# Two-layer conditional network on one core: the first loads divided between two DMA queues

## The chip, the cores and the metric

The kernel runs on one core of one Trainium2 chip. The metric is the device time of that core in microseconds (us), the median of several runs. TensorE (PE) multiplies matrices, VectorE (DVE), ScalarE (ACT) and GpSimd (POOL) work on elements, SyncE (SP) issues DMAs. ScalarE can issue DMAs too, on a queue of its own.

## What is computed

There are 4 batches of 512 tokens of width 256, and for each batch a vector of 8 numbers, `cond_8`. The first layer mixes eight weight matrices by these numbers, masks the mix and adds its result to x. The second layer is a mixture of experts with one shared expert; `cond_8` also picks and weighs two of the eight experts of a batch.

```python
# first layer, per batch b
masked_w = weight * mask[None, :, :]                 # 8 x 256 x 256
w_bot = jnp.einsum('bg,got->bot', y, masked_w)       # y = cond_8
x = x + jnp.einsum('bnt,bot->bno', x, w_bot) + bias
# second layer
w, sel = top_k(softmax(cond_8), 2); w = w / w.sum()
mlp = lambda x, g, u, d: (gelu(x @ g) * (x @ u)) @ d # 256 -> 1024 -> 256
x = x + sum(w[k] * mlp(x, *skill[sel[k]]) for k in (0, 1)) + mlp(x, *shared)
```

## The kernel before, in words

Everything is kept transposed: the 256 features lie in two halves (`hh`, `oh`) of 128 partitions, the 512 tokens of a batch along the free dimension. Each fp32 operand of a matmul is split into a high part (a cast to fp32r) and a low part (the rest), and a product is three matmuls. The high parts are cast by ScalarE, the low parts are formed by VectorE (x, h and the first-layer weight) or GpSimd (the weights of the second layer). An expert's weights are eight chunks of 128 x 768: 256 columns each for gate, up and down. The second layer walks over 24 chunks a batch (8 shared, 16 routed), `gate_up` two steps ahead of `down`. The order of the work of each engine is written out by hand, with semaphores between them.

Batch 0 has a way of its own ahead of these steps, and this is where the change lies:

- SyncE issues all big loads. Its list ahead of the batches (L218 to L231) is: weights 0 and 1 of the first layer (`l0_raw`, 256 KB each, L186), half 0 of x (`x_in`, 256 KB, L174), weights 2 and 3, half 1 of x, weights 4 to 7, two halves of the mask (L228), the eight chunks of the shared expert (`raw`, 384 KB each, L230), then, behind a wait for the splits of batch 0's x (L178), the x of batch 1. Each weight, each half of x and each chunk has a semaphore of its own.
- ScalarE issues one tiny load, `cond_row` (L469), copies `ident` (L471, with a table load ahead of it), scales `ident` by each of batch 0's eight numbers (`scale_ident`, L424, into `diag`, which lies in `out_sb`), casts the two halves of x (`split_x`, L401), loads the table for gelu (L481), casts the two halves of the mixed weight (`split_l0_0`, L405) and goes on to the shared chunks (`split_part`, L421).
- TensorE keeps itself busy with matmuls of zeros (`keep_warm`, L371), spreads `cond` over the partitions (L376), and mixes the second output halves of the eight weights with the scaled identities (`mix_l0`, L248). Between weights 5 and 6 it passes x through to the sum (`pass_x`, L256 and L258). Then come the first layer's own matmuls (`first_layer_0`, L266 and L270) and the second layer.
- VectorE mixes the first output halves of the weights, one instruction a weight (`combine_0`, L550 for weight 0 and L553), in the order 0 to 4, low part of x half 0 (L593), 5, low part of x half 1, 6, 7. Then it applies the masks (`apply_mask_0`, L563) to its own half and to TensorE's.

Weights of the first layer stay in `l0_raw` for all batches, so they are loaded once.

Of the kernel before, what the change touches and what calls it, by code (L numbers as in the profile page):

```python
# [25 lines left out]

def build(nc, xT, cond, l0_w, l0_mask, experts, shared, outT):
    B, _, HH, T = xT.shape
    G = l0_w.shape[0]
    E, CHUNKS, _, WC = experts.shape  # L30
    D = HH * P
    L0C = HH * D
# [14 lines left out]
    with ExitStack() as ctx:  # L47
        def sb(name, shape, dt=F32):
            return ctx.enter_context(nc.sbuf_tensor(name, shape, dt))
# [4 lines left out]
        def sem(name):  # L54
            return ctx.enter_context(nc.semaphore(name))
# [22 lines left out]
        l0_raw = sb("l0_raw", [P, G, L0C])  # L78
# [4 lines left out]
        x_in = sb("x_in", [P, HH, T])  # L83
# [39 lines left out]
        l0_in = [sem(f"l0_in{g}") for g in range(G)]  # L123
        mask_in = [sem(f"mask_in{oh}") for oh in range(HH)]
        x_loaded = [sem(f"x_loaded{hh}") for hh in range(HH)]
# [45 lines left out]
        @block.sync  # L171
        def _(sp):
            def load_x_half(b, hh):
                sp.dma_start(x_in[:, hh], xT[bass.ds(b, 1), :, hh].rearrange("a p t -> (a p) t")).then_inc(x_loaded[hh], 16)  # L174

            def load_x(b):
                if isinstance(b, int) and b == 1:
                    sp.wait_ge(x_hi_done, HH)  # L178
                    sp.wait_ge(x_lo_done, HH)
                else:  # L180
                    sp.wait_ge(x1_done, HH * b)
                for hh in range(HH):
                    load_x_half(b, hh)

            def load_l0(g):
                sp.dma_start(l0_raw[:, g], l0_w[g]).then_inc(l0_in[g], 16)  # L186

            def load_expert(b, j, e):


                sp.wait_ge(w_lo_done, ECH * b + CHUNKS + j - RAW_SLOTS + 1)
                src = experts[bass.ds(e, 1), j % CHUNKS].rearrange("a p w -> (a p) w")
                sp.dma_start(raw[:, j % RAW_SLOTS], src).then_inc(raw_in[j % RAW_SLOTS], 16)

            def expert_of(b, k):
                return sp.value_load(top_idx[0:1, bass.ds(b, 1), k], min_val=0, max_val=E - 1)

            def batch(b, with_next):

                if with_next and not isinstance(b, int):  # L200
                    load_x(b + 1)
                e = expert_of(b, 1)
                for j in range(CHUNKS, ECH):
                    load_expert(b, j, e)
                if with_next:
                    e = expert_of(b + 1, 0)
                    for j in range(CHUNKS):
                        load_expert(b + 1, j, e)
                for i, (hh, tokens) in enumerate(OUT_PIECES):
                    if with_next:  # L210
                        sp.wait_ge(out_done, len(OUT_PIECES) * b + i + 2)
                    elif i != 1:
                        sp.wait_ge(last_out_done, i + 1)
                    if with_next or i != 1:
                        dst = outT[bass.ds(b, 1), :, hh, tokens].rearrange("a p t -> (a p) t")
                        sp.dma_start(dst, out_sb[:, hh, tokens]).then_inc(stored, 16)

            sp.sem_inc(stored, 1)  # L218
            for g in range(2):
                load_l0(g)  # L220
            load_x_half(0, 0)
            for g in range(2, 4):
                load_l0(g)
            load_x_half(0, 1)
            for g in range(4, G):
                load_l0(g)
            for oh in range(HH):
                sp.dma_start(mask[:, oh], l0_mask[oh]).then_inc(mask_in[oh], 16)  # L228
            for c in range(CHUNKS):
                sp.dma_start(raw[:, c % RAW_SLOTS], shared[c]).then_inc(raw_in[c % RAW_SLOTS], 16)  # L230
            load_x(1)  # L231
            sp.wait_ge(indexed, B)
            e = expert_of(0, 0)
            for j in range(CHUNKS):
                load_expert(0, j, e)
            batch(0, True)
            with sp.Fori(1, B - 1) as b:
                batch(b, True)
            batch(B - 1, False)
            sp.wait_ge(stored, 16 * len(OUT_PIECES) * B + 1)  # L240
# [155 lines left out]
        def _(act):  # L396
# [70 lines left out]
                            split_x1(b + 1, s - L0_STEP - 2)  # L467

            act.dma_start(cond_row[:], cond).then_inc(cond_in, 16)  # L469
            act.wait_ge(ident_done, 2)  # L470
            act.copy(ident_r[:], ident[:]).then_inc(ident_r_done, 1)  # L471
            act.wait_ge(cond_ready, 1)
# [305 lines left out]
```

## Time and profile before

| | |
|---|---|
| median of 3 runs | 422.52 us (422.02 to 422.61) |
| the profiled execution, its own time | 422.13 us |
| its span in the trace | 420.0 us |
| TensorE matmuls busy | 414.6 us (99%) |
| VectorE, ScalarE, GpSimd busy | 189.6, 184.7 and 140.1 us |
| queue q1 (issued by SyncE) | 34.74 MB |
| queue q10 (issued by ScalarE) | 0.13 MB: the load of cond and one store at the end |

All times of the trace count from the start of the span. A busy time is the time in which an engine executes; the table says which engine is busiest, not what the others wait for. For that there are the list of waits, the chain of work that ended last, and the timelines of the engines.

### The profile page before, as it was taken

To read this page: it belongs to the slowest core of one execution; us is meant where nothing else is said; L and a number is where in the kernel's file an instruction comes from. 1 tells how busy PE (TensorE), PEld (TensorE's weight loads), DVE (VectorE), ACT (ScalarE), POOL (GpSimd) and SP (SyncE) were. 2 spreads that over 40 slices of the span, in tenths; PEclk is the share of its full clock that TensorE was granted. 3 is DMA by queue.
4 is the path that set the end of the run, shared out by engine and by line. 5 is a ranking of instruction groups with operands and counts; after the bars stand their busy time and mean duration, and the time that the engine had idled before them with its cause. 6 is when DMAs were issued, how large, how long until landed. Compare 5 with 4: busy or idle time off the path is not lost.

```text
span 420.0 us, 5319 instructions
## 1 busy us (share of the span) xinstructions
PE 414.6 (99%) x1818; PEld 341.2 (81%) x1818; DVE 189.6 (45%) x299; ACT 184.7 (44%) x306; POOL 140.1 (33%) x86
## 2 busy tenths in 40 slices
PE   8999999999999999999999999999999999999996
PEld 6778888888888888888888888888888888888885
DVE  3668654353445445345335554524434333343334
ACT  6676454463223535445222553535422435444431
POOL 1566545343001354435000344543300054443500
PEclk9999999999999999999999999999999999999999
DMA  7965232322011323223102132332300123210001
GB/s 267 357 202 156 96 113 75 114 71 80 0 59 41 108 80 113 81 70 112 37 0 101 37 112 75 112 81 69 112 0 8 43 75 113 80 34 0 2 0 50
DMA packets 14705, 35.05 MB, mean 83 GB/s; under 512 B 1634, under 2 KB 2914, under 8 KB 14690
## 3 DMA queue, kind: packets, MB, share of 16 engines
q1 hardware_dynamic: 14544, 34.74, 25.9%
q8 instruction: 7, 0.11, 0.1%
q10 hardware_dynamic: 146, 0.13, 0.1%
q14 instruction: 8, 0.07, 0.1%
HBM read 32.77 MB, written 2.10 MB: 83 GB/s over the span
## 4 chain that ended last, share of the span: by engine, by line
PE 96%; DMA 1%; SPq 1%; DVE 1%; issue 0%; DVEq 0%; ACT 0%
PE o_ps L338 30%; PE g_ps L317 21%; PE u_ps L317 21%; PE u_ps L323 10%; PE g_ps L323 10%; PE l_ps L282 1%; DMA l_raw<-l_w 1%; PE l_ps L351 1%; PE l_ps L287 1%; PE l_ps L266 1%; DVE l_first L553 0%; SPq L186 0%; PE g_ps L351 0%; PE l_ps L270 0%; SPq L174 0%
## 5 line engine op out<-in xcount | busy, mean ns | idle before, releaser
L714 POOL TENSOR_TENSOR ex_lo<-raw,ex_hi 128x768 fp32r<-128x768 f32 x64 | 123.3, 1926 | 240.8 <-ACT ex_hi L447 240.8
L438 ACT ACTIVATE gelu<-g_ps 128x512 f32<-128x512 f32 x96 | 57.4, 598 | 175.6 <-PE g_ps L323 175.4
L617 DVE SCALAR_TENSOR_TENSOR u_ps<-gelu,route_cur,u_ps 128x512 f32<-128x512 f32 x64 | 48.4, 755 | 125.4 <-ACT gelu L438 125.4
L622 DVE TENSOR_TENSOR h_lo<-u_ps,h_hi 128x512 fp32r<-128x512 f32 x96 | 66.3, 691 | 31.6 <-ACT h_hi L450 30.5
L450 ACT CAST h_hi<-u_ps 128x512 fp32r<-128x512 f32 x96 | 56.4, 587 | 37.1 <-DVE u_ps L612 18.5
L447 ACT CAST ex_hi<-raw 128x768 fp32r<-128x768 f32 x64 | 52.9, 827 | 0.0
L317 PE MATMUL g_ps<-x_hi,ex_hi 128*128 (+1 forms) x128 | 49.8, 389 | 0.0
L317 PE MATMUL g_ps<-x_hi,ex_lo 128*128 (+1 forms) x128 | 49.8, 389 | 0.0
L317 PE MATMUL u_ps<-x_hi,ex_hi 128*128 (+1 forms) x128 | 49.8, 389 | 0.0
L317 PE MATMUL u_ps<-x_hi,ex_lo 128*128 (+1 forms) x128 | 49.8, 389 | 0.0
L338 PE MATMUL o_ps<-h_hi,ex_hi 128*128 128x512 f32 x122 | 47.5, 389 | 0.0
L338 PE MATMUL o_ps<-h_lo,ex_hi 128*128 128x512 f32 x122 | 47.5, 389 | 0.0
L338 PE MATMUL o_ps<-h_hi,ex_lo 128*128 128x512 f32 x122 | 47.5, 389 | 0.0
L612 DVE TENSOR_TENSOR u_ps<-gelu,u_ps 128x512 f32<-128x512 f32 x32 | 22.2, 695 | 43.6 <-ACT gelu L438 43.6
L323 PE MATMUL u_ps<-x_lo,ex_hi 128*128 (+1 forms) x128 | 39.4, 389 | 0.0
L323 PE MATMUL g_ps<-x_lo,ex_hi 128*128 (+1 forms) x128 | 39.4, 389 | 0.0
L317 PEld LDWEIGHTS u_ps<-x_hi,ex_lo 128*128 128x128 f32 x128 | 24.0, 188 | 5.0
L317 PEld LDWEIGHTS g_ps<-x_hi,ex_lo 128*128 128x128 f32 x128 | 24.0, 188 | 5.0
L323 PEld LDWEIGHTS u_ps<-x_lo,ex_hi 128*128 128x128 f32 x128 | 24.0, 188 | 5.0
L317 PEld LDWEIGHTS g_ps<-x_hi,ex_hi 128*128 128x128 f32 x128 | 24.0, 188 | 5.0
L323 PEld LDWEIGHTS g_ps<-x_lo,ex_hi 128*128 128x128 f32 x128 | 24.0, 188 | 5.0
L317 PEld LDWEIGHTS u_ps<-x_hi,ex_hi 128*128 128x128 f32 x128 | 24.0, 188 | 5.0
(112 smaller groups left out, 556.1 us busy)
## 6 DMA issues: line engine op xcount, KB each, us to landing
raw<-experts SPq DMA_DIRECT2D x64, 384.0 KB, 3.1
raw<-shared SPq DMA_DIRECT2D x8, 384.0 KB, 7.5
l_raw<-l_w SPq DMA_DIRECT2D x8, 256.0 KB, 4.9
x_in<-xT SPq DMA_DIRECT2D x8, 256.0 KB, 3.5
outT<-out_sb SPq DMA_DIRECT2D x4, 256.0 KB, 2.1
outT<-out_sb SPq DMA_DIRECT2D x7, 128.0 KB, 2.0
mask<-l_mask SPq DMA_DIRECT2D x2, 128.5 KB, 5.7
outT<-out_sb ACTq DMA_DIRECT2D x1, 128.0 KB, 2.3
```

What stands on the lines that cost most here:

```text
L266: pe.matmul(l0_ps[:, oh], l0_hi[:, at:at + P], x[:, th], start=False, stop=False)
L282: pe.matmul(l0_ps[:, oh], w[:, at:at + P], x_hi[:, th], start=(th == 0 and w is l0_hi), stop=False)
L317: pe.matmul(ps, w[:, at:at + P], x1_at(x1_hi, b, hh), start=(hh == 0 and w is w_hi), stop=False)
L323: mm = pe.matmul(ps, w_hi[:, at:at + P], x1_at(x1_lo, b, hh), start=False, stop=(hh == HH - 1))
L338: mm = pe.matmul(o_ps[:, oh], w[:, at:at + P], x[:, s % H_SLOTS], start=(s == 0 and i == 0), stop=((closes or s == STEPS - 1) and i == 2))
L438: act.activation(gelu[:, s % 2], g_ps[:, s % 2], ACT.Gelu_apprx_tanh).then_inc(gelu_done, 1)
L447: act.copy(ex_hi[:, j % RING], raw[:, j % RAW_SLOTS]).then_inc(w_hi_done, 1)
L450: act.copy(h_hi[:, s % H_SLOTS], u_ps[:, s % 2]).then_inc(h_hi_done, 1)
L612: dve.tensor_tensor(u_ps[:, s % 2], gelu[:, s % 2], u_ps[:, s % 2], ALU.mult).then_inc(h_done, 1)
L617: dve.scalar_tensor_tensor(u_ps[:, s % 2], gelu[:, s % 2], route_cur[:, k:k + 1], u_ps[:, s % 2], ALU.mult, ALU.mult).then_inc(h_done, 1)
L622: dve.tensor_tensor(h_lo[:, s % H_SLOTS], u_ps[:, s % 2], h_hi[:, s % H_SLOTS].bitcast(F32), ALU.subtract).then_inc(h_lo_done, 1)
L714: pool.tensor_tensor(lo, raw[:, slot], hi.bitcast(F32), ALU.subtract).then_inc(w_lo_done, 1)
```

## The change

Five loads leave SyncE's list or move in it. ScalarE issues weight 1, weight 2, half 1 of x and weight 4, in this order, right behind its load of cond and ahead of its copy of `ident`. SyncE issues weight 0, half 0 of x, weights 3, 5 and 7, and weight 6 as the last (`G` is 8), then masks and shared chunks as before. Semaphores, buffers and all waits are the same.

```diff
             sp.sem_inc(stored, 1)
-            for g in range(2):
+            load_l0(0)
+            load_x_half(0, 0)
+            for g in range(3, G, 2):
                 load_l0(g)
-            load_x_half(0, 0)
-            for g in range(2, 4):
-                load_l0(g)
-            load_x_half(0, 1)
-            for g in range(4, G):
-                load_l0(g)
+            load_l0(G - 2)
             for oh in range(HH):
                 sp.dma_start(mask[:, oh], l0_mask[oh]).then_inc(mask_in[oh], 16)
...
             act.dma_start(cond_row[:], cond).then_inc(cond_in, 16)
+            act.dma_start(l0_raw[:, 1], l0_w[1]).then_inc(l0_in[1], 16)
+            act.dma_start(l0_raw[:, 2], l0_w[2]).then_inc(l0_in[2], 16)
+            act.dma_start(x_in[:, 1], xT[0, :, 1]).then_inc(x_loaded[1], 16)
+            act.dma_start(l0_raw[:, 4], l0_w[4]).then_inc(l0_in[4], 16)
             act.wait_ge(ident_done, 2)
```

## Rows read from the trace of the kernel before

**Rows 1.** TensorE's waits, whole span: us in total, times, longest us.
```profile
PE g_ps L371 <- POOL h_hi L724: 1.4, 1, 1.4
PE l_ps L266 <- ACT l_hi L405: 0.6, 1, 0.6
```

**Rows 2.** The chain that ended last, in time: start us, us, what.
```profile
3.66 5.30 DMA l_raw<-l_w
...
13.07 1.20 PE l_ps L266 x4
```

**Rows 3.** Timeline, VectorE: start us, us, instruction, idle before and releaser.
```profile
8.98 0.48 DVE L553 SCALAR_TENSOR_TENSOR l_first<-l_raw,cond_all,l_first 128x256 f32<-128x256 f32 x1 [1.23 <-DMA l_raw<-l_w]
9.38 0.68 DVE L593 TENSOR_TENSOR x_lo<-x_in,x_hi 128x512 fp32r<-128x512 f32 x1
...
10.98 1.07 DVE L553 SCALAR_TENSOR_TENSOR l_first<-l_raw,cond_all,l_first 128x256 f32<-128x256 f32 x2
```

**Rows 4.** Timeline, SyncE's DMA issues, 0 to 11 us.
```profile
0.86 0.86 SPq L186 DMA_DIRECT2D l_raw<-l_w  x2
1.76 0.43 SPq L174 DMA_DIRECT2D x_in<-xT  x1
...
3.66 1.91 SPq L186 DMA_DIRECT2D l_raw<-l_w  x4
...
6.78 4.08 SPq L230 DMA_DIRECT2D raw<-shared  x8
```

**Rows 5.** Single issues at 1.76, 3.66, 4.14, 6.78 us: KB, us to landing.
```profile
x_in<-xT SPq DMA_DIRECT2D x1, 256.0 KB, 4.1
...
l_raw<-l_w SPq DMA_DIRECT2D x1, 256.0 KB, 5.3
...
l_raw<-l_w SPq DMA_DIRECT2D x1, 256.0 KB, 5.5
...
raw<-shared SPq DMA_DIRECT2D x1, 384.0 KB, 5.9
```

**Rows 6.** Timeline, TensorE's matmuls, 5 to 13 us.
```profile
5.38 1.05 PE L248 MATMUL u_ps<-l_raw,out_sb 128*128 128x256 f32 x2
...
8.56 0.58 PE L371 MATMUL g_ps<-h_hi 128*128 128x512 f32 x1
9.09 1.35 PE L248 MATMUL u_ps<-l_raw,out_sb 128*128 128x256 f32 x4
10.10 0.58 PE L256 MATMUL l_ps<-x_hi,ident_r 128*128 128x512 f32 x1
...
11.12 0.50 PE L258 MATMUL l_ps<-x_lo,ident_r 128*128 128x512 f32 x1
11.45 1.02 PE L248 MATMUL u_ps<-l_raw,out_sb 128*128 128x256 f32 x4
```

**Rows 7.** Timeline, ScalarE (ACTq: its DMA issues), 0 to 14 us.
```profile
0.79 0.54 ACTq L469 DMA_DIRECT2D cond_row<-cond  x1
...
4.70 0.69 ACT L424 ACTIVATE out_sb<-ident,cond_all 128x128 f32<-128x128 f32 x2 [1.74 <-DVE cond_all L506]
...
7.21 0.60 ACT L401 CAST x_hi<-x_in 128x512 fp32r<-128x512 f32 x1
8.22 0.62 ACT L401 CAST x_hi<-x_in 128x512 fp32r<-128x512 f32 x1 [0.40 <-DMA x_in<-xT]
...
13.36 0.71 ACT L421 CAST sh_hi<-raw 128x256 fp32r<-128x256 f32 x2
```

**Rows 8.** The page's DMA queues: packets, MB, share of 16 engines.
```profile
q1 hardware_dynamic: 14544, 34.74, 25.9%
q10 hardware_dynamic: 146, 0.13, 0.1%
```

**Rows 9.** Three stretches: busy us by engine; last three columns PEclk, DMA share, GB/s.
```profile
1.75:2.50 0.75, 0.75 (x3) 0.56 (x3) 0.00 (x0) 0.75 (x1) 0.21 (x1) 1.00 0.31 101
2.50:3.50 1.00, 1.00 (x4) 0.55 (x2) 0.00 (x0) 0.45 (x2) 0.00 (x0) 1.00 1.05 404
3.50:5.00 1.50, 1.50 (x5) 1.00 (x4) 0.50 (x5) 0.30 (x1) 0.00 (x0) 1.00 0.71 209
```

## The prediction

> **What bounds the kernel now.** I read the busy times first: TensorE's is nearly the whole span (the table above). Then the list of what TensorE waited for: two waits in the whole execution, 1.4 us for GpSimd's zeros at the start and 0.6 us in front of the first layer's own matmuls (L266), and none behind them [rows 1]. So from the start of L266 at 13.07 us [rows 2] the rest of the span (420.0 - 13.1 = 406.9 us) is one run of matmuls, and whatever moves that start moves the end by the same amount, as long as no new wait appears behind it. The change touches only what happens ahead of 13.07 us.
>
> What sets 13.07 us? The chain of waits goes back from there over VectorE's combining of the eight first-layer weights (L553) to the landing of one load, which it follows from 3.66 us, the issue of weight 4 [rows 2]. The timeline of VectorE shows the same: it waits 1.23 us for a load ahead of 8.98 us and runs with no wait from there: weight 4, x split, weight 5, x split, weights 6 and 7, mask [rows 3]. This stretch, 13.07 - 8.98 = 4.09 us, is fixed work in a fixed order, so one landing decides: that of weight 4. It is the seventh load of SyncE's queue (weights 0 and 1, x half 0, weights 2 and 3, x half 1, weight 4). Its landing is issue plus time to landing: 3.66 + 5.3 = 8.96 us [rows 4, 5].
>
> TensorE is nearly as late on the same stretch, and that limits any gain. Its own mixing of the weights' second halves (L248) reaches weight 4 at 9.09 us, just as the warming matmul before it (8.56 + 0.58 = 9.14) ends, so it was not held by the load. From 9.09 its own work up to L266 is: weights 4 and 5 until 10.10 (the first x pass), four passes over x, weights 6 and 7 in 1.02 us. The fourth pass starts at 11.12 after a short wait for the x split; four passes at the pitch of the others (about 0.25 to 0.3) would be done by about 11.2, so L266 can't start before about 9.09 + 1.01 + 1.1 + 1.02 = 12.2 us [rows 6]. The most that earlier loads can give is thus 13.07 - 12.2, about 0.8 us, an estimate from these rows.
>
> **The change part by part.**
>
> (1) SyncE issues four loads fewer ahead of the masks and the shared chunks. Its issues follow each other at 0.48 us (four in 1.91 us from 3.66) [rows 4], so everything behind them is issued 4 x 0.48 = 1.9 us earlier. This alone brings nothing where the data path and not the issue is the limit: a weight lands 0.66 us after the one before (weight 5: 4.14 + 5.5 = 9.64, weight 4: 8.96), more than the 0.48 us between issues, and five us lie between issue and landing [rows 4, 5]. The first shared chunk, issued at 6.78, lands at 6.78 + 5.9 = 12.7 us, and ScalarE takes it up at 13.36, after L405 [rows 4, 5, 7]: 0.66 us of cover, and the same bytes lie ahead of it afterwards. Cost and gain zero. The second x loads wait at L178 for the x splits of batch 0 in both kernels, so they don't come into this stretch.
>
> (2) The order in which the bytes arrive. Loads move to a second queue; that the split is real is seen from the page, where the one load and the one store that ScalarE issues stand under q10, not q1 [rows 8]. Two queues that share the same DMA engines are nowhere busy at once in the trace of before, so this has to be bounded. One end: ScalarE's queue is served first when it has data; then weight 4 comes behind weight 0 and three loads of its own queue (weights 1, 2, x half 1) with a little of SyncE's, fifth or sixth instead of seventh: 0.66 to 1.3 us earlier. Other end: the queues share evenly, and ScalarE's is one load behind because its first issue is cond (0.79 to 1.33) while SyncE's weight 0 starts at 0.86 [rows 4, 7]; then weights 0, 3, 5, 7 and x half 0 of SyncE's queue go past before weight 4 is complete: ninth, so 2 x 0.66 = 1.3 us later. Even sharing with both queues in step makes it eighth, 0.66 us later, at 9.64. I take the eighth place, the middle of the even cases, since nothing in the trace gives one queue the preference.
>
> (3) The bubble in the early traffic. With one queue the DMA engines move 404 GB/s between 2.5 and 3.5 us and only 209 GB/s between 3.5 and 5.0, though SyncE has issued five or six loads by then [rows 4, 9]. It is the time of x half 0, the first load of another tensor: issued at 1.76 it lands at 1.76 + 4.1 = 5.86 [rows 4, 5]. Bytes not moved: (404 - 209) x 1.5 us = 292 KB, which at 404 GB/s are 0.72 us. If the bubble belongs to SyncE's queue, ScalarE's loads fill it and all later landings are 0.72 us earlier; if it lies in the DMA engines or the memory, nothing is gained. Bounds 0 and 0.72 us, with up to (404 - 101) x 0.75 us = 227 KB, 0.56 us, more if the slow start between 1.75 and 2.5 us belongs to the one queue too. I take 0.72: with the engines busy at a 0.71 share in that stretch against 1.05 before, they lacked work, and a second queue with work is what the change brings [rows 9].
>
> So weight 4: 8.96 + 0.66 - 0.72 = 8.90 us, that is 0.06 us earlier than now. Weights 5, 6 and 7 land in other orders, weight 6 last at 11.0 - 0.7; VectorE takes it at 10.98 [rows 3], so the cover is about 0.7 us and goes only if the bubble stays, when weight 4 is late too and moves VectorE's order with it.
>
> The Trainium skill speaks against (3): the page "DMA: Bandwidth & Descriptors", section "Issuing engines are not separate DMA queues", says that loads from several engines run on the same 16 DMA engines and interleave, and that issuing from several saves only the sequencer's issue time. By that rule the 0.72 us stays away and the sum is +0.66 us instead of about 0; it is the first rival below. The trace has a row on the issue time (0.48 us a load, hidden), and none on two queues at once.
>
> (4) ScalarE issues four more loads, before its table load and the copy of ident. One of SyncE's costs 0.48 us; ScalarE's only early one took 0.54 [rows 4, 7]. So 1.9 to 2.3 us. ScalarE idles 1.74 us ahead of its first scaling of ident at 4.70 [rows 7], which hides that much; 0.2 to 0.6 us spill over. Queued behind: eight scalings of ident, for which TensorE's L248 waits from 5.38 on, and the x copy that starts at 7.21. The second x copy waits 0.40 us for its load already (8.22) [rows 7], and VectorE doesn't need the first before 9.38 = 8.98 + 0.40, when it has been there since 7.8: 1.6 us of cover, so VectorE's chain takes nothing of it. TensorE's order moves by the spill: L266 not before 12.2 + 0.4 = 12.6, still under 13.07. Cost zero, but it lowers the greatest possible gain from 0.8 to 0.2 to 0.6 us.
>
> Sum: the start of L266 at 13.07 - 0.06 = 13.0 us, the span 420.0, the profiled execution 422.1 as before. The profiled one took 422.13 and the median of the runs is 422.52, so 0.4 us are added: 422.5 us.
>
> **The rivals.**
>
> (A) The bubble is not filled, and sharing is even. Weight 4 lands eighth at 9.64 (+0.68) or ninth at 10.30 (+1.34); VectorE, which waits for it, hands all of it on. 423.2 to 423.9 us. This is the slower side: it decides from the point where the landing of weight 4 passes 8.98 us. For it: the even pitch of 0.66 us a load once traffic is full. Against: the idle share of the engines in the bubble.
>
> (B) ScalarE's queue gets ahead, because SyncE's stalls on x half 0. Weight 4 lands sixth or earlier, by 8.3 us or before. Then VectorE is no longer last and TensorE's L248 order is: L266 at 12.4 to 12.8, 421.8 to 422.3 us. Its gain ends at TensorE's own work.
>
> (C) The two issuing engines hinder each other, so that a load costs ScalarE twice 0.48 us. Then 4 x 0.96 - 1.74 = 2.1 us spill, L248 starts at 7.5 instead of 5.38, and L266 not before 12.2 + 2.1 = 14.3: +1.2 us, 423.7 us. It decides from a spill over 0.8 us. TensorE would also idle for 2 us ahead of L248, whose first matmuls already run slower than the later ones (1.05 us for two at 5.38, 1.35 for four at 9.09) [rows 6]; what a longer pause there does is not in the trace.
>
> **How the numbers follow.** Forecast (start of L266 between -0.2 and +0.4 us): 0.45, with 422.3 to 422.9 as its own range. (A) 0.27, (B) 0.18, (C) 0.10. A measurement of this kernel tells 0.2%, 0.85 us, from no change. Faster by more needs the whole cap of 0.8 us and noise besides: 0.06, out of (B). Slower by more: the ninth place in (A), 0.13, and most of (C), 0.08, so 0.21. Same: 0.73. The range takes in (B) down to 421.7 and (A) nearly to its end, 423.7.
>
> **What would show it.** In the trace of after: q1 and q10 both busy between 2 and 8 us; weight 4 landing near 8.9; GB/s between 3.5 and 5.0 near 400 if step (3) holds, near 209 if (A) does; ScalarE's first scaling at 4.9 to 5.3, and over 6 if (C) holds; ahead of L266 a wait for ScalarE's L405 as now, or none with L248 right before it in (B). The forecast is wrong if TensorE waits anywhere behind L266 where it does not now, or if its matmuls ahead of it change their pace.

## The result and the profile after

The changed kernel took 423.74 us (median of 9 runs, 423.33 to 424.55), the one before 422.52 us (9 runs, 422.02 to 422.98). The ratio is 1.003, with a 95% interval of 1.0021 to 1.0038: slower by 1.2 us, a little past the upper end of the range (423.7). The profiled execution took 423.44 us with a span of 421.3 us, 1.3 us more than the 420.0 before.

Where the 1.3 us are is seen in TensorE's list of waits and in the chain, in that order. The waits of TensorE in the changed kernel (us in total, times, longest us; its line numbers are a few off those of before: L263 is L266, L245 is L248, L554 is L553):

```profile
PE g_ps L368 <- POOL h_hi L725: 1.4, 1, 1.4
PE l_ps L263 <- ACT l_hi L402: 0.6, 1, 0.6
PE l_ps L255 <- DVE x_lo L594: 0.2, 1, 0.2
```

Nothing is new behind the first layer. The chain that ended last, over the head of the kernel (start us, us, what):

```profile
2.73 7.55 DMA l_raw<-l_w
...
10.31 0.48 DVE l_first L554
...
13.94 0.41 ACT l_hi L402
...
14.39 1.18 PE l_ps L263 x4
```

It has the shape of [rows 2]: one load, VectorE's fixed order, ScalarE's cast, the first layer. But the load is now one that ScalarE issues at 2.73 us, earlier than SyncE's 3.66, and it takes 7.55 us to land instead of 5.30. Weight 4 is there at 10.28 us instead of 8.96, and the first layer's matmuls start at 14.39 instead of 13.07. From there the two traces are the same length: 421.3 - 14.39 and 420.0 - 13.07 are both 406.9 us. VectorE's timeline (it answers to [rows 3]; idle before and releaser in brackets) shows the same wait, now 1.65 us, and behind it the same order at the same pace:

```profile
10.31 0.48 DVE L554 SCALAR_TENSOR_TENSOR l_first<-l_raw,cond_all,l_first 128x256 f32<-128x256 f32 x1 [1.65 <-DMA l_raw<-l_w]
10.71 0.68 DVE L594 TENSOR_TENSOR x_lo<-x_in,x_hi 128x512 fp32r<-128x512 f32 x1
```

ScalarE (answers to [rows 7]) issues its five loads from 0.80 to 3.2 us, and its first scaling starts at 4.77 instead of 4.70:

```profile
2.73 0.50 ACTq L470 DMA_DIRECT2D l_raw<-l_w  x1
...
4.77 0.69 ACT L421 ACTIVATE out_sb<-ident,cond_all 128x128 f32<-128x128 f32 x2
```

How the two queues share is in the view of the DMA queues. Between 1.8 and 3.3 us (queue: packets, MB, share of 16 engines) only SyncE's queue moves data, though ScalarE has issued weight 1 at 1.38; between 6 and 8 us both move nearly the same:

```profile
q1 hardware_dynamic: 180, 0.34, 69.5%
```

```profile
q1 hardware_dynamic: 221, 0.41, 55.5%
q10 hardware_dynamic: 210, 0.38, 49.5%
```

So ScalarE's queue starts about a load late (SyncE's has moved 0.34 MB by then, 1.3 loads) and then gets half. Weight 4, the last of its four big loads, has to wait until SyncE's queue has passed weight 0, half 0 of x and weights 3, 5 and 7. Issue plus time to landing puts them at 3.7, 5.0, 7.4, 8.8 and 10.1 us, and weight 6 at 10.8: weight 4, at 10.28, is the ninth of ten, where it was the seventh.

### The profile page after: what moved, and what is told of

Its sections match the earlier page's. It is cut to its first block, busy times and chain, and to the rows that moved or that the text cites. A ratio compares the mean times of both kernels' runs of the same rounds, so it can differ in the third digit from the quotient of the medians.

```text
span 421.3 us, 5319 instructions
## 1 busy us (share of the span) xinstructions
PE 415.6 (99%) x1818; PEld 342.1 (81%) x1818; DVE 189.5 (45%) x299; ACT 184.6 (44%) x306; POOL 140.3 (33%) x86
## 4 chain that ended last, share of the span: by engine, by line
PE 96%; DMA 2%; DVE 1%; ACTq 0%; issue 0%; DVEq 0%; ACT 0%
PE o_ps L335 30%; PE g_ps L314 21%; PE u_ps L314 21%; PE g_ps L320 10%; PE u_ps L320 10%; DMA l_raw<-l_w 2%; PE l_ps L279 1%; PE l_ps L348 1%; PE l_ps L284 1%; PE l_ps L263 0%; DVE l_first L554 0%; PE g_ps L348 0%; PE l_ps L267 0%; DVEq L47 0%; ACTq L466 0%
```

## The experiments

The theory, called "place": the second queue costs nothing by itself; the kernel is later because weight 4 lands two places later, and the order of arrival alone decides, down to the point where TensorE's own work would. The rival, called "second queue": what costs is the sharing of the DMA engines and ScalarE's issues. Each edit is given as the order of the loads ahead of the masks (numbers are weights, x0 and x1 the halves of x). For comparison:

```
before    SyncE: 0 1 x0 2 3 x1 4 5 6 7
changed   SyncE: 0 x0 3 5 7 6           ScalarE: cond 1 2 x1 4
```

**One queue, weight 4 ninth.**

```diff
 # SyncE
-0 1 x0 2 3 x1 4 5 6 7
+0 1 x0 2 3 x1 5 7 4 6
```

> The kernel before with one queue, weight 4 issued ninth, behind weights 5 and 7 (the place it took in the changed kernel). Theory 'place': the landing of weight 4 decides and the second queue costs nothing by itself; it lands at about 10.3 us (8.96 + 2 x 0.66), the first layer's matmuls start at 14.4 instead of 13.07, and the kernel takes 1.3 us more, 423.8. Rival 'second queue': the extra time comes from sharing and from ScalarE's issues; then weight 4 matters less here and the time is under 423.0.

423.5 us (10 runs), ratio 1.0026 (1.0016 to 1.0037). With one queue and no change on ScalarE the kernel is as late as the changed one (1.21 us over the median before in the same comparison, 422.29; the changed one has 1.22): weight 4 lands 5.4 us behind its issue at 4.61, at 10.0 us, and the first layer's matmuls start at 14.14. VectorE's wait:

```profile
10.05 0.49 DVE L555 SCALAR_TENSOR_TENSOR l_first<-l_raw,cond_all,l_first 128x256 f32<-128x256 f32 x1 [2.20 <-DMA l_raw<-l_w]
```

The order of arrival makes the loss without a second queue.

**Two queues, the weights in order.** ScalarE keeps three of its four big loads.

```diff
-SyncE: 0 x0 3 5 7 6      ScalarE: cond 1 2 x1 4
+SyncE: 0 x0 3 4 5 6 7    ScalarE: cond 1 2 x1
```

> Two queues, but weight 4 back in SyncE's queue: SyncE issues 0, x half 0, 3, 4, 5, 6, 7, ScalarE 1, 2, x half 1. Theory 'place': weight 4 lands where weight 5 landed in the changed kernel, at 8.8 us, the first layer's matmuls start at 12.9 and the time is 422.3 (no more than 422.7). Rival 'second queue': the time stays near the changed kernel's, 423.5 or more.

422.15 us (10 runs), ratio 1.0002 (0.9992 to 1.0013); start of the first layer's matmuls 13.00 us. With the second queue still there the loss is gone. VectorE waits elsewhere now, for weight 2 of ScalarE's queue, and takes 2, 3 and 4 in one go (timeline):

```profile
7.74 1.66 DVE L555 SCALAR_TENSOR_TENSOR l_first<-l_raw,cond_all,l_first 128x256 f32<-128x256 f32 x3 [0.99 <-DMA l_raw<-l_w]
```

**The changed kernel with weights 4 and 5 exchanged.** Four loads on ScalarE, as in the change.

```diff
-SyncE: 0 x0 3 5 7 6      ScalarE: cond 1 2 x1 4
+SyncE: 0 x0 3 4 7 6      ScalarE: cond 1 2 x1 5
```

> The changed kernel with weights 4 and 5 exchanged between the queues: SyncE 0, x half 0, 3, 4, 7, 6, ScalarE 1, 2, x half 1, 5. Still four loads on ScalarE's queue. Theory 'place': weight 4 lands at 8.8 us, weight 5 at 10.3; VectorE now waits for weight 5, by 0.4 to 0.5 us, instead of for weight 4 by 1.3; the first layer's matmuls start at 13.3 to 13.5 and the time is 422.7 to 423.0. Rival 'four issues on ScalarE or the shared queues cost': it stays at 423.7.

422.3 us (10 runs), ratio 0.9998 (0.9986 to 1.0011), better than expected. Weight 4 lands at 8.4 us, weight 5 at 10.06 (2.73 + 7.3), and VectorE waits 0.57 us for it; the matmuls start at 13.18 us. The last of ScalarE's four loads is again the ninth to land. Four issues on ScalarE cost nothing that is seen, and exchanging two loads takes the whole loss back.

**ScalarE's first big load ahead of cond.**

```diff
 # ScalarE
-cond 1 2 x1 4
+1 cond 2 x1 4
```

> The changed kernel with ScalarE's load of weight 1 ahead of its load of cond, so that ScalarE's queue gets its first big load 0.5 us earlier. Theory 'late start of the queue makes weight 4 ninth instead of eighth': weight 4 lands at 9.6 to 9.9 us instead of 10.3 and the time is 423.1 to 423.4. Rival 'the place is set by something else than the order of issue': weight 4 stays at 10.3, 423.7.

423.58 us (10 runs), ratio to its own runs of before 1.0022 (1.0013 to 1.0032). In the trace ScalarE's queue moves 0.22 MB between 1.8 and 3.3 us, where it moved none, and weight 4 lands 6.9 us behind 2.68, at 9.6 us: eighth, one place (0.66 us) earlier, and the matmuls start at 13.72. In this execution, then, the head start of ScalarE's queue turns the ninth place into the eighth. The time does not confirm it. The profiled execution took 422.82 us, the second fastest of the ten, and the median of 423.58 lies above the 423.1 to 423.4 expected and is not told apart from the changed kernel's (the intervals of the ratios overlap). How most executions of this kernel lose some 0.9 us is thus not seen. The load of cond itself lands later here, and TensorE waits 0.6 us for it, until 4.4 us; VectorE still waits 1.55 us for weight 4 behind that, so this wait is not what sets 13.72.

**What is next behind weight 4.** One queue, x half 1 behind weight 4.

```diff
 # SyncE
-0 1 x0 2 3 x1 4 5 6 7
+0 1 x0 2 3 4 x1 5 6 7
```

> One queue, half 1 of x and weight 4 change places (weight 4 sixth). Weight 4 lands at 8.3 us. If its landing alone decided, the first layer's matmuls would start at 12.4 (-0.7, 421.8). Theory 'next in line': weight 5 stays eighth (9.64), VectorE waits for it, and the start is 12.7 to 12.8 (-0.3, 422.2).

422.45 us (10 runs), ratio 1.0 (0.9991 to 1.001); the matmuls start at 13.36 us, later than in the kernel before. Weight 4 landed at 8.87 us, not 8.3: in this execution the slow stretch of the DMA engines lasted until 6.5 us at least (below). VectorE then waits 0.28 us for weight 5 at 10.26, as "next in line" says, but from an arrival that was late for another reason. A gain of 0.3 us is not confirmed.

**The bubble.** One queue, x half 0 as the fifth load.

```diff
 # SyncE
-0 1 x0 2 3 x1 4 5 6 7
+0 1 2 3 x0 4 x1 5 6 7
```

> One queue, order 0, 1, 2, 3, x half 0, 4, x half 1, 5, 6, 7: what makes the bubble of 209 GB/s between 3.5 and 5.0 us? Theory 'first load of another tensor': it moves with x half 0, to about 5.0 to 6.3 us, and 3.5 to 5.0 runs near 400 GB/s. Theory 'supply at the start' (the loads' descriptors can't be made faster than this so early): it stays between 3.5 and 5.0, near 209 GB/s. Time by either: weight 4 lands at 8.3, x half 0 at 7.6 instead of 5.9, the start of the first layer's matmuls at 12.6 to 12.9, 422.1 to 422.4.

421.97 us (10 runs), ratio 0.9993 (0.9984 to 1.0003), the matmuls at 13.45 us. Stretches of 1.5 us (the last two columns: share of the DMA engines, GB/s):

```profile
3.50:5.00 1.50, 1.50 (x5) 1.00 (x4) 0.50 (x5) 0.31 (x2) 0.00 (x0) 1.00 1.00 350
5.00:6.50 1.50, 1.50 (x5) 1.18 (x4) 1.24 (x5) 1.50 (x7) 0.00 (x0) 1.00 0.82 223
```

In the kernel with x half 1 behind weight 4, where x half 0 is third, the same stretches have 210 and 231 GB/s. By GB/s the slowest stretch comes later when x half 0 does, which would speak for the first load of another tensor. The landings do not bear it out. Most loads land 0.6 to 0.7 us apart, and one pause stands out in each profile. With x half 0 third the pause ends with its landing; with x half 0 fifth it falls between the landings of weights 2 and 3 (1.76 + 3.6 = 5.34 and 2.24 + 5.3 = 7.54 us), and x half 0, behind them in the queue, follows 0.8 us later. Neither theory is shown, and the slow stretch differs much between executions.

> The kernel with one queue and x half 0 as the fifth load, once more and with more rounds, since its median was 0.3 us under the kernel before. If that was chance, the ratio is 1.0 within its interval; its first profile (first layer's matmuls at 13.45 us, against 13.07 and 13.14) speaks for chance.

422.48 us (12 runs), ratio 1.0 (0.9991 to 1.0008): the lower median of the first time was chance. 303 GB/s between 3.5 and 5.0 and 253 between 5.0 and 6.5 us: again the later stretch is the slower one, less clearly. The longest pause between landings is now the one ahead of weight 2, from 4.21 to 1.77 + 4.4 = 6.17 us, nearly where the kernel before has it (4.26 to 5.89). What makes the slow stretch stays open.

**The two kernels once more**, one profile each.

> The changed kernel itself, a second profile: how far do the landing of weight 4 (10.28 us) and the moment when TensorE's first matmuls get to their later pace differ between executions? If the landing is a matter of the order of issue, it is 10.0 to 10.5 again.

> The kernel before itself, a second profile: weight 4 lands at 8.8 to 9.1 us again, with 200 to 230 GB/s between 3.5 and 5.0 us; if TensorE's matmuls of zeros get their later pace at another moment than 7.3 us, that moment is not set by the kernel.

The kernel before: weight 4 at 9.03 us, span 420.1. The bubble is smaller (276 GB/s, where 200 to 230 were expected), and this brings nothing to weight 4:

```profile
3.50:5.00 1.50, 1.50 (x5) 1.00 (x4) 0.50 (x5) 0.31 (x2) 0.00 (x0) 1.00 0.95 276
```

The changed kernel: weight 4, ninth again, lands only at 11.2 us, 8.4 us behind its issue; the order of issue doesn't bound it to 10.5 as expected. The matmuls start at 15.30 and the span is 422.2, again 406.9 us more. TensorE now waits for loads too:

```profile
PE u_ps L245 <- DMA l_raw<-l_w: 1.6, 2, 1.1
```

The changed kernel's runs reach from 423.33 to 424.55 us; this execution (424.35) is one of the late ones. Why its loads came 0.9 us later is open: the GB/s of the two stretches (283 and 350 against 314 and 348) differ by 0.04 MB, which is 0.1 us at 400 GB/s (an estimate).

**A version meant to beat both.** ScalarE's late queue carries only what is needed late enough.

```diff
-SyncE: 0 1 x0 2 3 x1 4 5 6 7
+SyncE: 0 2 x0 4 5 6 7    ScalarE: cond 1 3 x1
```

> A version meant to beat the kernel before: SyncE 0, 2, x half 0, 4, 5, 6, 7, ScalarE 1, 3, x half 1. In the kernel with the weights in order VectorE was held by weight 2 (landed 7.7 us) and not by weight 4. Theory 'place': weight 2 lands by 6.2 us, weight 3 by 7.7, weight 4 at 8.6; VectorE takes weight 4 at 8.6 and the first layer's matmuls could start at 12.7, where TensorE's own mixing (done at 12.6 to 12.9) holds them as well: 12.7 to 13.0, 421.9 to 422.3, a gain of 0.1 to 0.4 us that only the trace can show. Rival: the first x half, now third on SyncE's queue, delays weight 4 and nothing is gained, 422.4.

421.91 us (12 runs), ratio 0.9987 (0.9978 to 0.9996): 0.56 us faster than the kernel before (422.47 in the same comparison), just clear of noise, in one comparison that was not repeated (the 0.3 us of x half 0 as the fifth load went away when it was). Weight 2 lands at 4.9 us, weight 4 at 8.69, and the first layer's matmuls start at 12.80 us. The list of waits shows none ahead of them, and TensorE's own mixing ends only at 11.70 + 1.02 = 12.72 us; but the chain that ended last still goes from weight 4 over VectorE and ScalarE's cast, which ends at 12.75:

```profile
2.23 6.45 DMA l_raw<-l_w
...
8.71 0.48 DVE l_first L555
...
12.34 0.41 ACT l_hi L404
...
12.80 1.19 PE l_ps L265 x4
```

Both paths end within 0.05 us of each other, so here earlier loads alone would bring hardly more.

All profiles together. The last column is span minus start. The landing of weight 4 alone does not order the rows. In the four profiles marked * VectorE has to wait once more, for weight 5: it takes that at 10.08 to 10.36 us, and the start follows 3.1 us behind. In the other eight it runs on without a wait from weight 4, which it takes at 8.71 to 11.21 us, and the start follows 4.08 to 4.09 us behind:

| kernel | weight 4 lands | start of L266 | span | rest |
|---|---|---|---|---|
| two_queues_w2_early | 8.7 | 12.80 | 419.8 | 407.0 |
| two_queues_w4_in_order | 8.6 | 13.00 | 420.0 | 407.0 |
| before / again | 8.96 / 9.03 | 13.07 / 13.14 | 420.0 / 420.1 | 406.9 / 407.0 |
| one_queue_x0_fifth / again * | 9.0 / 8.7 | 13.45 / 13.17 | 420.4 / 420.1 | 406.9 / 406.9 |
| changed_w4_w5_swapped * | 8.4 | 13.18 | 420.2 | 407.0 |
| one_queue_x1_behind_w4 * | 8.87 | 13.36 | 420.3 | 406.9 |
| changed_cond_second | 9.6 | 13.72 | 420.7 | 407.0 |
| one_queue_w4_ninth | 10.0 | 14.14 | 421.1 | 407.0 |
| changed / again | 10.28 / 11.2 | 14.39 / 15.30 | 421.3 / 422.2 | 406.9 / 406.9 |

## Why the prediction was wrong, step by step

**What bounds the kernel: right.** In all twelve profiles the rest behind L266 is 406.9 to 407.0 us (the table above). In the changed kernel the landing of weight 4 decides, with 4.1 us from VectorE's taking it to the start of L266 (14.39 - 10.31), as in the kernel before. One reading was wrong, without effect on the forecast: TensorE was held by the loads too. Its weight loads (PEld) for weights 4 and 5, in the kernel before, come 0.1 us behind the landings at 8.96 and 9.64 us, after idle time:

```profile
9.06 0.30 PEld L248 LDWEIGHTS u_ps<-l_raw,out_sb 128*128 128x128 f32 x2 [0.34 <-issue]
9.75 0.30 PEld L248 LDWEIGHTS u_ps<-l_raw,out_sb 128*128 128x128 f32 x2 [0.39 <-issue]
```

In the second profile of that kernel, where no load holds it, TensorE needs 3.25 us from the last matmul of zeros (9.71) to the end of its mixing (12.96). From 8.56 this gives 11.8 and not 12.2 us, and a cap of about 1.25 us instead of 0.8 for that execution (an estimate).

**Step (1), the masks and chunks: right.** They were issued about 2 us earlier and the traces show no gain from it.

**Step (2), the place: this is the step that failed.** Its bounds held the result, the value chosen did not. The even sharing was right (0.41 and 0.38 MB between 6 and 8 us), and the text itself said that ScalarE's queue is a load behind because cond goes first. That gives the ninth place; the eighth was taken as "the middle of the even cases", which no row supported. The term was +1.34 us and was put at +0.66. With cond behind weight 1 the eighth place came in the one profile taken, at 9.6 us against the 9.64 worked out for it.

**Step (3), the bubble: mis-sized.** -0.72 us was taken, and for weight 4 it was 0: ninth place without any gain is 10.30 us, and it landed at 10.28 and, in the second profile, at 11.19. That the first agrees to 0.02 us is luck in part, as the second shows. Neither sign that was named for the stretch came: 314 GB/s, where near 400 or near 209 was to decide. The second queue did bring more traffic: by 9 us 2.33 to 2.43 MB had been moved in the six profiles with two queues and 2.04 to 2.29 MB in the six with one. Between the two kernels' first profiles the difference is 0.20 MB, about 0.5 us at 400 GB/s (an estimate). But it did not reach weight 4, and why is open. In the second profile of the kernel before 276 GB/s were moved in the stretch with one queue, and weight 4 came no earlier either. The last of the eight weights lands at 10.5 to 11.7 us in the six profiles with two queues (mean 10.9) and at 10.7 to 11.7 in the six with one (mean 11.25): some 0.35 us, not clear of the spread. The idle share of the engines was one execution's, and it was read as if it were the kernel's. The rule of the Trainium skill, that issuing from several queues saves only issue time ("DMA: Bandwidth & Descriptors", section "Issuing engines are not separate DMA queues"), was the better guide for weight 4: its landing is that of the ninth place without a gain. The trace agrees that the loads interleave (0.41 and 0.38 MB between 6 and 8 us).

**Step (4), ScalarE's issues: right, even a little less.** The first scaling began at 4.77, so 0.07 us spilled over where 0.2 to 0.6 were expected: its big loads cost 0.36 to 0.50 us each. The rival (C), that the two issuing engines hinder each other, is refuted by these durations.

**The rivals.** (A) is what happened, in its ninth place, with 423.9 us against 423.74 measured. It had 0.27 and its slower half 0.13. (B) did not happen: ScalarE's queue had no data before 3.3 us and landed its first big load, weight 1, at 5.3 us, behind half 0 of x at 5.0. Its end, TensorE's mixing as the bound at 12.4 to 12.8 us, is neither confirmed nor refuted: in the last experiment the mixing ended at 12.72 and the chain from weight 4 at 12.75.

**The sum** had two errors in the same direction, 1.34 - 0.66 = 0.68 us for the place and 0.72 us for the bubble, 1.40 together; the start of L266 was forecast at 13.01 us and measured at 14.39, 1.38 later. Because the terms were both taken on the favourable side, their sum was the forecast, and the upper end of the range stopped short of the full (A).

## What to carry to other kernels

Before loads are divided between two queues, write down the order in which they arrive if the queues share evenly and the second starts late, and set it against the order in which they are used: here the last load of the short queue arrived two places later, and exchanging two loads took the whole loss back. A queue's shape at the start differs from execution to execution, so a gap in it is no sure gain; look at a second profile or leave it at zero. With a fixed run of work behind it, the landing that is waited for last, read from the trace, gives the end of the kernel to 0.1 us; which load that is can change with the order.

## What the runs showed of the hardware that was not expected

The second queue's first data came 2.0 us behind its first big issue (issued at 1.38 us, none moved on q10 until 3.3 us), and 1.5 to 2.0 us in the other profiles where cond goes first. When ScalarE's big load was issued first, at 0.80 us and ahead of SyncE's at 0.86, its queue moved 0.22 MB in the same time, and SyncE's first data came at 2.4 us instead of 1.9. The lag is thus not a property of ScalarE's queue; it looks like a matter of the order of issue over both queues, which was not tried further.

TensorE's first matmuls run at about half the later pace in every profile (the pair of L248 and the matmul of zeros behind it start 0.49 us apart at 5.4 us and 0.24 at 8.3 in the kernel before), and the moment when this ends is not set by the kernel. The matmul of zeros at about 8.5 us takes 0.58 us in the kernel before [rows 6] and 0.99 us in its second profile, whose timeline has these lines (the PEclk column of the stretches reads 1.00 in both):

```profile
8.43 0.99 PE L371 MATMUL g_ps<-h_hi 128*128 128x512 f32 x1
...
13.14 0.73 PE L266 MATMUL l_ps<-x_hi,l_hi 128*128 128x512 f32 x2 [0.17 <-ACT l_hi L405]
```

The later change of pace used up TensorE's slack (its wait ahead of L266 is 0.17 us instead of 0.6) and cost nothing here. It does lower what earlier loads can give: about 1.25 us in the first execution (estimated above) and 0.17 us in the second, so the cap of 0.8 us in the prediction, read from one execution, was no property of the kernel.
